# Router choices moved to ScalarE, small products on other PSUM banks, and a new order of the expert stage

## The reference

```python
x = einsum('bnd,de->bne', patches(imgs), W) + b            # 16 x 36 x 192
q, k, v = split(x @ w_qkv.T)                               # 12 heads of 64
q = q * rsqrt(norm(q, axis=1) + 1e-8)   # axis=1: the norm is taken over the heads
k = k * rsqrt(norm(k, axis=1) + 1e-8)
h = layernorm(x + softmax(q @ k.T / scale) @ v @ w_out.T + b_out)
logits = h @ Wr + br                                       # 8 experts
vals, idx = top_k(logits, 2); p = softmax(vals)
gu = h @ Wgu + bgu                                         # all 8 experts
act = (max(min(up, 7), -7) + 1) * gate * sigmoid(1.702 * gate)
out = layernorm(h + sum over the two chosen experts of p * (act @ Wd + bd))
```

## Time and profile before

| What | Value |
|---|---|
| time, median of 3 runs (lowest, highest) | 186.21 us (185.9, 187.57) |
| the profiled execution: time / span of its core | 187.39 / 185.7 us |
| PE busy | 161.9 us (87%) |
| VectorE busy | 131.5 us (71%) |
| GpSimd busy | 90.2 us (49%) |
| ScalarE busy | 85.4 us (46%) |
| mean granted clock of TensorE | 0.947 of full |

### The profile page before, as it was taken

One profiled execution on the slowest core, in us unless ns is written; L12 is line 12 of the kernel. 1 busy time (PEld: TensorE's weight loads), 2 busy tenths in 40 slices (PEclk: granted clock), 3 DMA queues, 4 the chain that ended last, 5 costly groups with the idle time before them and its releaser, 6 DMA issues.

```text
span 185.7 us, 3415 instructions
## 1 busy us (share of the span) xinstructions
PE 161.9 (87%) x1252; PEld 142.8 (77%) x1252; DVE 131.5 (71%) x290; ACT 85.4 (46%) x156; POOL 90.2 (49%) x96
## 2 busy tenths in 40 slices
PE   7799998988985999689989899979879999999940
PEld 2498897977764897668769687859779999999930
DVE  0387799779496558998978588888965276376743
ACT  3367964645933446246444531724306244444610
POOL 7600592897354885375768484233316233144301
PEclk9999999999996699999965969999999999999997
DMA  6999975004200202011000000000000000000101
GB/s 175 321 312 253 282 208 175 0 0 97 78 0 2 88 2 88 0 33 52 4 0 0 5 0 0 4 0 0 0 4 0 0 4 4 0 0 4 48 0 48
DMA packets 4400, 10.62 MB, mean 57 GB/s; under 512 B 608, under 2 KB 1312, under 8 KB 4384
## 3 DMA queue, kind: packets, MB, share of 16 engines
q1 hardware_dynamic: 4384, 10.41, 19.5%
...
## 4 chain that ended last, share of the span: by engine, by line
PE 44%; DVE 30%; issue 9%; ACT 5%; DMA 5%; SPq 3%; POOL 1%; POOLq 0%; DVEq 0%; ACTq 0%
DVE sel L794 5%; DMA stage<-w_qkv_b 5%; PE ps L1139 4%; DVE reg_q L680 4%; PE ps L976 4%; PE ps L980 3%; PE ps L977 3%; PE ps L978 3%; PE ps L979 3%; PE ps L1080 3%; PE ps L1122 3%; DVE reg_p L662 3%; PE ps L1104 2%; DVE mx_r L722 2%; DVE reg_x L689 2%
## 5 line engine op out<-in xcount | busy, mean ns | idle before, releaser
L352 POOL TENSOR_TENSOR reg_r<-reg_q,reg_r 128x288 fp32r<-128x288 f32 x22 | 17.8, 813 | 30.0 <-ACT reg_r L536 30.0
L301 POOL TENSOR_TENSOR reg_w<-stage,reg_w 128x768 fp32r<-128x768 f32 x12 | 23.5, 1972 | 12.5 <-ACT reg_w L403 12.5
L817 DVE TENSOR_SCALAR reg_q<-ps,bup 128x288 f32<-128x288 f32 x24 | 12.3, 514 | 15.9 <-PE ps L980 15.9
L536 ACT ACTIVATE reg_r<-reg_q 128x288 fp32r<-128x288 f32 x24 | 10.6, 444 | 24.9 <-DVE reg_q L832 19.9
L330 POOL TENSOR_TENSOR reg_p<-reg_p,rinv 108x648 f32<-108x648 f32 (+1 forms) x12 | 14.8, 1233 | 14.7 <-DVE rinv L734 14.7
L1139 PE MATMUL ps<-wout,oT 128*108 128x192 f32 (+1 forms) x72 | 15.5, 373 | 1.7 <-DVE lg L773 1.4
L1139 PEld LDWEIGHTS ps<-wout,oT 128*108 128x108 f32 (+1 forms) x72 | 13.0, 193 | 3.0 <-issue 1.8
L976 PE MATMUL ps<-reg_r,reg_w 128*128 128x288 f32 x48 | 14.9, 310 | 0.1
L528 ACT ACTIVATE reg_q<-ps,sm 128x288 f32<-128x288 f32 x24 | 11.9, 496 | 6.0 <-PE ps L980 5.3
L722 DVE TENSOR_REDUCE mx_r<-ps 108x6 fp32r<-108x648 f32 (+1 forms) x12 | 9.1, 755 | 7.5 <-PE ps L1080 7.5
L403 ACT ACTIVATE reg_w<-stage 128x768 fp32r<-128x768 f32 x14 | 11.8, 845 | 5.2 <-DMA stage<-w_gu_a 1.9
...
## 6 DMA issues: line engine op xcount, KB each, us to landing
...
```

The lines of the kernel that those rows point to most:

```text
L301: nc.gpsimd.tensor_tensor(dst[:, 1, :], raw, f(dst[:, 0, :]), ALU.subtract).then_inc(s_wlop, 1)
L352: nc.gpsimd.tensor_tensor(acts[:, n % NACT, 1], act_f[:, n % 4], f(acts[:, n % NACT, 0]), ALU.subtract).then_inc(s_alo, 1)
```

## The change

- Router: `router_top` is cut in `read_logits` and `rank`; the gap is now a tensor_scalar. `router_weights` on VectorE keeps two tensor_scalars (1+e and -1-e) and a reciprocal of both. New `choose(g)` on ScalarE: two Abs (distance of an iota row from each index), one Copy with a scale, two Relu with bias and scale that write the two one-hot rows side by side (16 columns in place of 8). So the one-hot and bias tables get four row blocks in place of two: two more affine selects on GpSimd at the start.
- Banks: h1 transposed and the logits of groups 0 to 3 go to bank 6, and the router rows to bank 7 (except group 2). Expert units use banks 0 to 3 only (`b` is 0 or 2), all spread weights go to bank 6, the down accumulators to banks 4 and 5.
- Order: `h1_transpose`, `h1_evac`, `h1_lo`, `logits`, `w_transpose` and what follows stand a step or more later; `q_norm(1)` stands before the loop, `q_norm(2)` to `q_norm(5)` in the odd steps 1 to 7, ahead of `sum_recip` (before: even steps, at the end). `gap_exp` stands behind `probs` and `k_norm` in even steps.
- Experts: `expert` is cut in `gate_up` and `spread`, and its VectorE part in `up_in`, `weigh` and `expert_act`; until unit 15 the spread of a unit comes after the gate and up products of the next. `residual(0)` stands after `gate_up(3)`, and `down(0)` after `gate_up(4)`: one `down` per unit from there.

The core of the diff (not shown: the same bank names in other readers, semaphore names, tiles):

```diff
+        L_BANK, HT_COL, LG_COL = 7, 0, W_COL + GRP
+        ACC = 4
+        B_BANK = O_BANK
+
+        def ht_bank(g):
+            return O_BANK if g < 4 else L_BANK
+
+        def wt_bank(g):
+            return O_BANK if g == 2 else L_BANK
...
-            return 3 * (place(n) % 2)
+            return 2 * (place(n) % 2)
...
+            for i, row in enumerate((0, E, 32, 32 + E)):
+                fill(onehot3, -row, [[-1, E], [0, 128]], 1.0, 5 + i)
...
-                if k >= 5 and k % 2 == 1 and k // 2 - 2 < NG:
-                    gap_exp(k // 2 - 2)
-                if k < NU:
-                    probs(k)
-                if k % 2 == 0 and 2 + k // 2 < NG:
+                probs(k)
+                if k in (0, 2, 4, 6):
                     k_norm(2 + k // 2)
+                if k >= 6 and k % 2 == 0:
+                    gap_exp(k // 2 - 3)
...
+            gap_exp(3)
+            root(5, SIZES[5], s_ve, s_rstd)
             act_lo(0)
-            root(5, SIZES[5], s_ve, s_rstd)
             act_lo(1)
             act_lo(2)
+            act_lo(3)
+            gap_exp(4)
+            act_lo(4)
+            act_lo(5)
             gap_exp(5)
...
+            def choose(g):
+
+                n = SIZES[g]
+                iota = sm[0:n, C_IOTA:C_IOTA + 8]
+                act.wait_ge(s_idx, g + 1)
+                if g >= 1:
+                    act.wait_ge(s_w2, 2 * g)
+                for j in range(2):
+                    nc.scalar.activation(far[0:n, j, :], iota, ACT.Abs, bias=rt[0:n, j:j + 1], scale=-1.0)\
+                        .then_inc(s_far, 1)
+                act.wait_ge(s_p1, g + 1)
+                nc.scalar.activation(p2[0:n, :], rt[0:n, 4:6], ACT.Copy, scale=rt[0:n, 3:4]).then_inc(s_p2, 1)
+                act.wait_ge(s_far, 2 * g + 2)
+                act.wait_ge(s_p2, g + 1)
+                if g >= 1:
+                    act.wait_ge(s_wt, g)
+                for j, prob in enumerate((rt[0:n, 4:6], p2[0:n, :])):
+                    nc.scalar.activation(w2[0:n, 0:64].rearrange("p (a e) -> p a e", a=2)[:, :, 8 * j:8 * j + 8],
+                                         far[0:n, j:j + 1, :].to_broadcast([n, 2, 8]), ACT.Relu,
+                                         bias=prob[:, 0:1], scale=prob[:, 1:2]).then_inc(s_w2, 1)
...
+                if k in (9, 11):
+                    w2_hi(k // 2 - 4)
...
-                if k >= 6 and k % 2 == 0 and k // 2 - 3 < NG:
-                    w2_hi(k // 2 - 3)
+                if k >= 7 and k % 2 == 1:
+                    choose(k // 2 - 3)
...
+            expert(0)
+            expert(1)
+            o_evac(11)
             h1_evac(4)
-            w2_hi(3)
-            expert(0)
-            o_evac(11)
-            expert(1)
+            expert(2)
+            w2_hi(2)
+            choose(3)
             act_hi(0)
-            expert(2)
+            expert(3)
             act_hi(1)
...
+                if g >= 1:
+                    dve.wait_ge(s_w2, 2 * g)
+                nc.vector.tensor_scalar(rt[0:n, 2:3], top[0:n, 1:2], top[0:n, 0:1], None, ALU.subtract)\
+                    .then_inc(s_gap, 1)
...
-                nc.vector.tensor_scalar_add(rt[0:n, 6:7], rt[0:n, 3:4], 1.0).then_inc(s_rs, 1)
-                dve.wait_ge(s_idx, g + 1)
-                nc.vector.tensor_scalar(sel[0:n, 0], iota, rt[0:n, 1:2], rt[0:n, 3:4], ALU.is_equal,
-                                        ALU.mult).then_inc(s_sel0, 1)
-                dve.wait_ge(s_rs, g + 1)
-                nc.vector.reciprocal(rt[0:n, 4:5], rt[0:n, 6:7]).then_inc(s_p1, 1)
-                dve.wait_ge(s_sel0, g + 1)
-                nc.vector.scalar_tensor_tensor(out=sel[0:n, 1], in0=iota, scalar=rt[0:n, 0:1], in1=sel[0:n, 0],
-                                               op0=ALU.is_equal, op1=ALU.add).then_inc(s_sel1, 1)
-                dve.wait_ge(s_sel1, g + 1)
-                dve.wait_ge(s_p1, g + 1)
-                if g >= 1:
-                    dve.wait_ge(s_wt, g)
-                nc.vector.tensor_scalar(w2[0:n, 0:64].rearrange("p (a e) -> p a e", a=2)[:, :, 0:8],
-                                        sel[0:n, 1:2, :].to_broadcast([n, 2, 8]), rt[0:n, 4:5], None,
-                                        ALU.mult).then_inc(s_w2, 1)
+                nc.vector.tensor_scalar(rt[0:n, 6:7], rt[0:n, 3:4], 1.0, None, ALU.add).then_inc(s_rs, 1)
+                nc.vector.tensor_scalar(rt[0:n, 7:8], rt[0:n, 3:4], -1.0, -1.0, ALU.mult, ALU.add).then_inc(s_rs, 1)
+                dve.wait_ge(s_rs, 2 * g + 2)
+                nc.vector.reciprocal(rt[0:n, 4:6], rt[0:n, 6:8]).then_inc(s_p1, 1)
...
+            q_norm(1)
...
                 if k + 1 < NU:
                     row_max(k + 1)
-                if k >= 5 and k % 2 == 1 and k // 2 - 2 < NG:
-                    router_top(k // 2 - 2)
-                if k >= 4 and k % 2 == 0 and k // 2 - 2 < NG:
+                if k in (9, 11):
+                    w2_lo(k // 2 - 4)
+                if k >= 4 and k % 2 == 0:
                     ln1(k // 2 - 2)
-                if k < NU:
-                    sum_recip(k)
+                if k in (1, 3, 5, 7):
+                    q_norm(k // 2 + 2)
+                sum_recip(k)
                 if k == 0:
-                    q_norm(1)
                     v_evac(5)
-                if k >= 4 and k % 2 == 0 and k // 2 - 2 < NG:
+                if k >= 6 and k % 2 == 0:
+                    read_logits(k // 2 - 3)
+                    rank(k // 2 - 3)
+                if k >= 7 and k % 2 == 1:
+                    router_weights(k // 2 - 3)
+                if k >= 5 and k % 2 == 1:
                     h1_lo(k // 2 - 2)
-                if k >= 5 and k % 2 == 1 and k // 2 - 2 < NG:
-                    router_weights(k // 2 - 2)
-                if k % 2 == 0 and 2 + k // 2 < NG:
-                    q_norm(2 + k // 2)
...
+            up_in(0)
+            read_logits(3)
+            rank(3)
+            up_in(1)
+            router_weights(3)
             h1_lo(4)
+            up_in(2)
+            w2_lo(2)
+            ln1_stats(5)
+            weigh(0)
+            expert_act(0)
+            ln1(5)
+            up_in(3)
+            weigh(1)
+            expert_act(1)
+            weigh(2)
+            expert_act(2)
+            h1_lo(5)
+            up_in(4)
+            weigh(3)
+            expert_act(3)
+            read_logits(4)
+            rank(4)
+            up_in(5)
+            weigh(4)
+            expert_act(4)
+            router_weights(4)
+            read_logits(5)
+            up_in(6)
+            weigh(5)
+            expert_act(5)
             w2_lo(3)
-            expert_in(1)
-            router_top(4)
-            expert_in(2)
-            ln1_stats(5)
...
-            for n in range(7, 2 * NT):
-                expert_in(n)
-                if n == 7:
+            for n in range(9, 2 * NT):
+                if n == NT + 4:
+                    weigh(n - 1)
+                    expert_act(n - 1)
+                if n < NT + 4:
+                    up_in(n)
+                    weigh(n - 1)
+                    expert_act(n - 1)
+                else:
+                    expert_in(n)
...
+                if u >= 4 and u % 2 == 0:
+                    pe.wait_ge(s_h1lo, u - 2)
                 if u >= 5 and u % 2 == 1:
-                    pe.wait_ge(s_w2lo, (u - 3) // 2)
+                    pe.wait_ge(s_lg, (u - 3) // 2)
...
-                    pe.wait_ge(s_h1lo, 2 * g)
-                    pe.wait_ge(s_lg, g)
+                if g >= 3:
+                    pe.wait_ge(s_w2lo, g - 2)
+                if g == 5:
+                    pe.wait_ge(s_h1lo, 10)
...
+                pe.wait_ge(s_oev, min(2 * g + 4, NU))
...
+                pe.wait_ge(s_h1lo, 2 * (g + 1) if g < 4 else 2 * NG)
+                if g < 4:
+                    pe.wait_ge(s_oev, 2 * g + 5)
+                else:
+                    pe.wait_ge(s_lg, g)
...
+                pe.wait_ge(s_w2, 2 * g + 2)
+                if g < 2:
+                    pe.wait_ge(s_h1, g + 3)
+                elif g == 2:
+                    pe.wait_ge(s_oev, NU)
+                else:
+                    pe.wait_ge(s_lg, NG)
+                    pe.wait_ge(s_w2lo, g)
+                nc.tensor.transpose(ps[:, wt_bank(g), W_COL:W_COL + n], w2[0:n, :], ident[0:n, 0:n]).then_inc(s_wt, 1)
...
+                if n == 0:
+                    pe.wait_ge(s_oev, NU)
+                    pe.wait_ge(s_lg, 4)
+                    pe.wait_ge(s_w2lo, 3)
+                else:
+                    pe.wait_ge(s_b, n)
...
-                    pe.wait_ge(s_oev, NU)
+                    pe.wait_ge(s_ptev, NU)
+                    pe.wait_ge(s_w2lo, 3)
+                else:
                     pe.wait_ge(s_w2lo, NG)
-                    pe.wait_ge(s_lg, NG)
...
+                if k in (9, 11):
+                    w_transpose(k // 2 - 4)
...
-                if k >= 4 and k % 2 == 0 and k // 2 - 2 < NG:
```

(57 more changed lines are left out.)

171 lines of the change are left out of this document (81 added, 90 removed).

## The result

The changed kernel takes 179.09 us (median of 4 executions, 177.98 to 180.52) against 186.31 us for the kernel before beside it (185.9 to 187.57): ratio 0.9606, 95% interval 0.952 to 0.9693. On a second chip it took 178.53 against 187.82 us, ratio 0.9531 (0.9478 to 0.9584). Forecast were 178.0 us and a range of 172.5 to 184.0.

A forecast was written before the change was run, and what follows sets the result against it. PE and VectorE were taken to bound it together, VectorE standing until GpSimd pauses. Stage gains of 12.5 us gave span 173.2; 3.3 for clock and 1.0 for hops made 177.5, with time outside and profiling offset 178.0 us, range 172.5 to 184.0.

The forecast's parts named there:

- Query norms: Attention steps 1 to 3: subtract_max(2) no longer waits behind q_norm(2); gain 2.9 us, and 0.3 us in step 3.
- Steps 4 to 8: Attention's two full-clock stretches: project's 1.43 us wait goes, gain 1.4 us; rank's cast stands behind probs, second gain 0.4 us.
- Steps 8 to 11: Last attention steps up to the first gate product: gains 3.2 and 1.7 us, some 4.4 of these 4.9 from clock.
- The clock: Half speed cost 6.5 us in all; half of it, 3.3 us, was taken as kept (bounds 0 and 6.5).
- the rival on the clock: Pauses ahead of step 3 and in steps 8 to 11 bring clock falls that take the gain: 184.1 us, chance 0.14.
- ScalarE: Five small router operations per group at 0.2 us each, 6 us in all, hidden: cost taken as 0.
- that rival: If Abs or Relu needs table loads, each choose costs 2.6 us per group on ScalarE: 191 us, chance 0.04.
- Experts: Expert stage: one down per unit ends PE's idle time, gain 4.1 us less 1.5 for new waits, 2.6 net.
- Start and tail: Two more selects at the start (2.33 us) hidden in GpSimd idle time, cost 0; the 7.8 us tail stays.
- The signs: Expected in the trace: first gate product at 102 to 105, last down near 170, q_norm 0.8 us in two steps.
- VectorE stays the bound: Standing time moves to rank and q_norm(4), and the down chain misses in ten units: 183.5 us, chance 0.14.
- too shy: No clock fall and no missed down, so the replay forecasts too little gain: 173.2 us, chance 0.12.

The follow-up runs named there:

- e4_before_qnorm: The kernel before with the query norms alone moved (q_norm(1) ahead of the loop, the others ahead of sum_recip in odd steps): 181.74 us, ratio 0.9739 to before.
- e8_qnorm_back: The changed kernel with the query norms of groups 1 to 3 back behind sum_recip in the even steps: 180.57 us, ratio 0.9622 to before.
- e1_rank_later: The changed kernel with rank moved from the end of the even step to the next odd step, behind w2_lo: median 182.04 us, ratio 0.9571 to before.
- e10_small_later: The changed kernel with rank(1), rank(2) a step later, the third expert unit behind its transposes, GpSimd's w_lo copies one a step: 174.09 us, ratio 0.9313 to before.
- e7_before_choose: The kernel before with only the router's one-hot rows made on ScalarE instead of VectorE: 182.82 us, ratio 0.9751 to before.
- e9_before_both: The kernel before with query norms moved and router rows on ScalarE, without the other banks, later step or early down products: 178.37 us, ratio 0.9545.
- e5_after_again: The changed kernel, unchanged, run once more on a second chip: 178.53 us, ratio 0.9531 to before.
- e12_small_later_q2: e10_small_later with q_norm(4) put behind sum_recip(5) and q_norm(2) behind sum_recip(1): 172.47 us, ratio 0.9223 to before.

## Why the prediction was right, point by point

The sum was right (8.2 us less of span forecast, 7.9 measured), its terms only in part, so a part of the hit is luck. The terms for the stages add up to 12.5 us, measured to 9.2; that the sum came out even so is owed to the 4.3 us that I took off for the clock and for hops. With the clock that was lost already inside the 9.2, nothing had to come off but 1.36 us at the start, which I had at nothing.

- **Query norms.** Forecast 2.9 and 0.3. Measured from `subtract_max(1)` to `(3)` 9.95 us before and 6.65 after, 3.3, and 0.2 in step 3. `subtract_max(2)` starts 2.41 us behind `subtract_max(1)` (forecast 55.2 - 52.96 = 2.2), and PE's wait ahead of `p_transpose(1)` is 1.47 us (forecast 1.7). `e4_before_qnorm` has the same 3.3 us there (6.64 from 52.70 to 59.34) and is 5.5 us faster in all; `e8_qnorm_back` takes only 2.0 back, and in its profiled execution, where the clock stayed up, these two steps took 7.88 us.
- **Steps 4 to 8.** Forecast 1.4 and 0.4; measured 10.74 to 9.19 and 10.31 to 9.78, 1.55 and 0.53. The 1.43 us wait is gone. The cast in step 6 took 0.70 us, 0.5 more than alone where I had 1.0 more, and PE waited 0.53 us for `probs(6)`.
- **Steps 8 to 11.** Forecast 3.2 and 1.7; measured 1.06 and 1.2. This step failed. I priced `rank`'s cast for step 6 only, behind `probs` and `gap_exp`, and named no wait in step 8; there it stood 2.98 us, behind `probs`, `gap_exp` and `w_lo` in a row. And I looked for what it holds up in `probs`, not in `w2_lo` two places behind it, for which `project(3)` now waits. `e1_rank_later` moves `rank` alone, and both it and `e10_small_later` take 8.95 us for these steps where the changed kernel takes 12.14; my replay had 10.0.
- **The clock.** Forecast kept 3.3 us; of the four stretches of the earlier trace rows below 0.95 one is left, 0.87 of 12.14 us, some 1.6. I feared a fall behind the pause ahead of step 3; none came. Against the rival on the clock I named a pause of 1.43 us with no fall behind it, and passed over one of 1.28 us ahead of 93.73 in the kernel before, behind which the clock was 0.60 until 102.25.
- **ScalarE.** I took 0.2 us for each of the five operations, from a row for another operation. Measured over the whole run, by the groups of lines of the changed kernel:

```profile
L536 ACT ACTIVATE far<-sm,rt 108x8 f32<-108x8 f32 (+1 forms) x12 | 2.9, 292 | 0.4 <-DVE rt L830 0.4
L545 ACT ACTIVATE w<-far,rt 108x16 f32<-108x16 f32 (+1 forms) x6 | 2.4, 399 | 0.5
L545 ACT ACTIVATE w<-far,p 108x16 f32<-108x16 f32 (+1 forms) x6 | 2.3, 384 | 0.0
L539 ACT ACTIVATE p<-rt 108x2 f32<-108x2 f32 (+1 forms) x6 | 1.7, 287 | 1.7 <-DVE rt L838 1.7
```

  9.3 us of work in place of 6, and the move paid all the same: `e7_before_choose` gains 5.0. The Trainium skill (ScalarE: Activation LUTs, What ACT_TABLE_LOAD costs) has 186 ns for an activation, 93 more for each per-partition operand and 0.833 for each column, by which this Relu would take 0.385 us, an estimate. The trace agrees, with 0.384 and 0.399. No table load came beside those of before (five in each profile), so that rival is out.
- **Experts.** Forecast 4.1 less 1.5. Measured from the first gate product to the end 73.36 before and 72.02 after, 1.3. The sum was off by a factor of two, and the reason was wrong: that the early down products give VectorE "the PE time that it lacked". `e9_before_both`, without them, takes 71.14. What shortens the experts is `choose`: `e7_before_choose`, which has no other part of the change, takes 71.14 us, with VectorE busy for 44.57 in place of 47.74, and `e4_before_qnorm`, which lacks it, 73.26. The 1 us wait of `project(5)` came as forecast (1.01), waits of the down chain did not: `spread` waits 0.25 and 0.72 us.
- **Start and tail.** The first `subtract_max` came 1.36 us later in the profiled execution (51.14 against 49.78); it stands at 50.14 in that of `e5_after_again` and between 49.52 and 51.02 in the others. What delayed it in that one isn't shown. The tail kept its 7.8 us.
- **The signs.** The first gate product came at 105.82 (forecast 102 to 105), the last `down` ended at 170.04 (near 170). The granted clock over attention was 0.97. `q_norm` took 0.8 us in two of the steps (0.83 and 0.82).

Of the rivals, "VectorE stays the bound" had a mechanism that came (standing time at `rank` and `q_norm(4)`, 2.98 and 2.72 us), at about half its 5 us: attention fell 2.7 us short in steps 8 to 11. The 173.2 of "too shy" is near what `e10_small_later` and `e12_small_later_q2` take, but those are other kernels, not this one without clock falls.
